# First attention of a five-phase layer kernel: output stored by batch, more key and square buffers, SP's queue from a list, new orders on all five engines

## The chip, the cores and the metric

The kernel runs on one NeuronCore of a Trainium2 chip. The metric is the time of one execution on the device in microseconds (us); lower is better. The engines are named as the profile names them: PE (matmul), DVE (VectorE), ACT (ScalarE), POOL (GpSimd), and SP, whose queue issues nearly all DMA transfers.

## The reference, cut to what matters

Two layers over 32 batches of 56 tokens with 256 features. Each layer is a cross-attention to a context of 1500 rows and a feed-forward part. The change touches the first attention alone:

```
q = (ln(x) @ Wq + bq)  -> 16 heads of 128, rmsnorm
k = (ctx @ Wk + bk)    ->  4 heads of 128, rmsnorm   (each serves 4 heads of q)
v = (ctx @ Wv + bv)    ->  4 heads of 128
probs = softmax(q k^T / sqrt(128) + mask)      # 56 x 1500 per head
x = x + (probs @ v) @ Wo
```

## The kernel before, in words

The phases run one after the other: queries of the first attention (`q0_phase`), the first attention itself (`attn0_phase`), its output projection with the router, the experts, the second attention and the last feed-forward part. Each phase ends with a barrier of all engines.

`attn0_phase` keeps float32 accuracy by splitting values into a high and a low float16 part; every product is then three matmuls (`three_products`, lines 111 to 113). A batch has 1500 context rows, held as 12 tiles of 125 rows. The attention does not project the values: it mixes the context rows themselves with the probabilities, and multiplies the result by Wv afterwards. The work is cut into steps with a letter and a number, and each engine has a list of these steps in `ORDER0`:

- `D0` to `D3`: a quarter of a batch's context is split; ACT writes the high part `ch` (line 713), POOL the low part `cl` (line 848).
- `K0` to `K11`: PE projects the keys of one context tile into a PSUM bank `ps_w`; DVE adds the bias and writes it to the key buffer `kb` (line 788).
- `q0` to `q11`: POOL squares a key tile into `ksq` (line 856). `Q0` to `Q5`: DVE sums the squares of two tiles (line 776). `N0` to `N5`: POOL takes the power -1/2 (lines 863 and 867) and scales the two key tiles in place (line 873).
- `R0` to `R11`: PE transposes a normalised key tile (line 899); ACT writes the high part `kTh` (line 718), DVE the low part `kTl` (line 794).
- `S0` to `S7`: for two heads at once PE makes the scores `ps_s`, DVE masks them and takes the maximum (line 806), ACT takes the exponential (line 728). `I`: DVE inverts the sum (lines 812, 815). `H`: ACT writes the high part of the probabilities `ph` (line 735). `L`: DVE writes the low part `pl` (line 820). SP then transposes both by DMA (line 627) to `pTh` and `pTl`.
- `P0` to `P23`: PE mixes the context; six steps make one group of four heads, each step is 12 matmuls. `G0` to `G3`: ACT (line 741) and DVE (line 826) split the result.
- `O0` to `O3` on PE, `Z0` to `Z3` on ACT (line 747) and DVE (line 830): multiplication by Wv, bias, and the output tile `ot`.

`rounds` walks such a list once per turn. In turn b the attention steps belong to batch b (with `<` to batch b-1) and the key steps `K`, `R`, `q`, `Q`, `N` to batch b+1, `D` to batch b+2; `>` means one batch later still. So while PE attends to one batch it prepares the keys of the next. Turns come in a hardware loop of six, four passes of it, with the turns before and after written out.

SP's queue has no list: `step` (lines 641 to 668) issues per turn the 16 transposes of the probabilities, four pairs of context loads (`load_ctx`, lines 582 and 583), the transposes of the context in two halves (`turn_ctx`, line 597), their store for the second attention (`keep_ctx`, line 606), the loads of the queries (`load_q`, line 616) and, every second turn, the store of the output (line 634). SP waits in the order of this code: an instruction whose data is late holds all that stand behind it.

The output tile `ot` holds the outputs of two batches, interleaved so that a row of it is one run of memory. There is one such tile, so `Z0` of an even batch waits until the store of the pair before it has landed. `kb` has four tiles: `K` of tile n waits for `R` of tile n-4. `ksq` has two: `q` of a new pair waits until DVE has summed the pair before.

Of the kernel before, what the change touches and what calls it, by code (L numbers as in the profile page):

```python
# [12 lines left out]
ds = bass.ds  # L13
# [157 lines left out]
def q0_phase(nc, g, io):  # L171

    with phase(nc) as (ctx, a):
# [304 lines left out]
def rounds(eng, steps, attend, work):  # L478

    def turn(batch):  # L480
        for kind, n, off in steps:
            lead = {"D": 2, "K": 1, "R": 1, "q": 1, "N": 1, "Q": 1}.get(kind, 0)
            at = moved(batch, off + lead)
            if exists(at, B):
                (work if lead else attend)(kind, n, at)

    count = (B - 4) // ROUND
    for b in (-2, -1, 0):
        turn((b, b % ROUND, b // ROUND))
    with eng.Fori(0, count) as i:  # L490
        for k in range(1, ROUND + 1):
            turn((ROUND * i + k, k % ROUND, i + k // ROUND))
    for b in range(ROUND * count + 1, B + 1):
# [13 lines left out]
def attn0_phase(nc, g, io):  # L507
# [6 lines left out]
    HT = KT // 2  # L514
    PS = 256.0
    PW = 2 * RP
    with phase(nc) as (ctx, a):
# [28 lines left out]
        ot = a.sb("a_ot", [128, 2, NH, 2, S], F16)  # L546
# [12 lines left out]
        stored = a.sem("a_stored")  # L559
# [6 lines left out]
        def _(sp):  # L566
# [52 lines left out]
            def turn(tile, r):  # L619

                G, h, k = tile[0], r // 2, r % 2
                wait(sp, s["mix_done"], NKV * G + h - 1)
                passed(sp, sp_gate)
                for n, (p, pT, ready) in enumerate(((ph, pTh, "p_hi"), (pl, pTl, "p_lo"))):
                    sp.wait_ge(s[ready], NR * G + r + 1)
                    passed(sp, sp_gate)
                    sp.dma_start_transpose(out=pT[:, h % 2, :, k], in_=p[:, k].rearrange("q k c -> q (k c)"))\
# [1869 lines left out]
```

## Time and profile before

| what | value |
|---|---|
| median of 3 runs | 4904.94 us (4901.27 to 4908.27) |
| profiled execution | 4904.49 us, its span 4902.4 us |
| busy over the span | PE 79%, DVE 72%, POOL 56%, ACT 49% |
| the first attention | about 280 us to 2719 us of the span |
| TensorE's granted clock, mean | 0.905 of full speed |

The profiled execution's own time is 2.1 us longer than its span, and 0.5 us below the median. PE's row of the profile is "3748999899899989999999720886159999999945": slices of 122.6 us with the busy share in tenths. The long stretch of 8 and 9 from the fourth slice on is the first attention. A matmul's span is modelled and runs into the next one's, so PE's idle time is best read from the views that name waits.

### The profile page before, as it was taken

What the parts mean: (1) busy time and instruction counts of PE and PEld (TensorE: products, weight loads), DVE (VectorE), ACT (ScalarE), POOL (GpSimd) and SP (SyncE); (2) the same over time, 40 slices, a digit from 0 to 9 for tenths busy, and PEclk for the clock granted to TensorE, in tenths of its full rate; (3) what the DMA queues carried; (4) which work ended last, traced back from release to release, by engine and by line L of the source; (5) the groups of instructions that cost most, each with busy time, mean ns of one, the idle gap of its engine ahead of it and who ended that gap; (6) DMA issues with size and microseconds to landing.
All of it is one profiled execution on the core that took longest, in us unless ns stands there. A gap on an engine that the chain in (4) does not pass through costs nothing. (4 is left out here: it accounts for less than half of the span.)

```text
span 4902.4 us, 104372 instructions
## 1 busy us (share of the span) xinstructions
PE 3888.0 (79%) x34578; PEld 2966.4 (61%) x34579; DVE 3509.9 (72%) x5413; ACT 2405.4 (49%) x3575; POOL 2762.2 (56%) x2176
## 2 busy tenths in 40 slices
PE   3748999899899989999999720886159999999945
PEld 2426777676677667677777710775137767677734
DVE  4847777777777777777777263344778888888967
ACT  1325555455455555555555113332137777777743
POOL 2566677676676666677774125334635555555532
PEclk9869999999999999999999965898579999999966
DMA  5246667677666666766775536555345444444410
GB/s 206 83 118 141 157 150 150 148 152 156 149 149 146 157 142 156 153 147 157 161 155 115 177 103 200 130 138 147 113 119 132 118 123 118 124 123 122 116 46 26
DMA packets 1276100, 664.62 MB, mean 136 GB/s; under 512 B 1095841, under 2 KB 1202977, under 8 KB 1271182
## 3 DMA queue, kind: packets, MB, share of 16 engines
q1 hardware_dynamic: 1247422, 617.09, 52.3%
q0 software_dynamic: 9216, 22.03, 1.4%
q10 hardware_dynamic: 19008, 19.40, 1.2%
q8 instruction: 290, 4.75, 0.4%
q14 instruction: 164, 1.34, 0.1%
HBM read 188.99 MB, written 146.01 MB: 68 GB/s over the span
## 5 line engine op out<-in xcount | busy, mean ns | idle before, releaser
L111 PE MATMUL a_pa<-a_pTh,a_ch 125*128 125x224 f16 x3072 | 802.2, 261 | 13.3 <-issue 11.2
L1896 POOL TENSOR_TENSOR b_pTl<-b_pe,b_pTh 125x1344 f16<-125x1344 f32 x192 | 539.5, 2810 | 483.6 <-ACT b_pTh L1955 460.2
L113 PE MATMUL a_pa<-a_pTh,a_cl 125*128 125x224 f16 x3072 | 802.1, 261 | 0.0
L112 PE MATMUL a_pa<-a_pTl,a_ch 125*128 125x224 f16 x3072 | 801.8, 261 | 0.0
L856 POOL TENSOR_TENSOR a_ksq<-a_kb 125x512 f32<-125x512 f32 x384 | 479.0, 1247 | 345.9 <-DVE a_kb L788 263.7
L873 POOL TENSOR_TENSOR a_kb<-a_kb,a_rk 125x512 f32<-125x512 f32 x384 | 546.3, 1423 | 68.8 <-POOL a_kb L873 34.5
L728 ACT ACTIVATE a_pr<-a_pr,a_nmax 112x1500 f32<-112x1500 f32 x256 | 395.4, 1545 | 322.5 <-DVE a_nmax L806 321.0
L735 ACT ACTIVATE a_ph<-a_pr,a_inv 112x1500 f16<-112x1500 f32 x256 | 396.4, 1548 | 285.9 <-DVE a_inv L815 285.8
L820 DVE SCALAR_TENSOR_TENSOR a_pl<-a_pr,a_inv,a_ph 112x1500 f16<-112x1500 f32 x256 | 480.9, 1878 | 67.0 <-ACT a_ph L735 66.5
L2001 DVE TENSOR_REDUCE b_mx<-b_ps 112x3 f32<-112x1500 f32 x256 | 439.1, 1715 | 96.3 <-PE b_ps L2078 94.9
L806 DVE CUSTOM_DVE_ANT_0 a_pr<-a_ps,a_mask 112x1500 f32<-112x1500 f32 x256 | 438.9, 1715 | 67.2 <-PE a_ps L113 58.5
L1948 ACT ACTIVATE b_pe<-b_pt 125x448 f32<-125x448 f32 x768 | 393.4, 541 | 165.0 <-PE b_pt L2100 159.7
L899 PE MATMUL a_pw<-ident,a_kb 125*128 125x125 f32 x1536 | 237.7, 278 | 153.8 <-POOL a_kb L873 113.0
L1955 ACT ACTIVATE b_pTh<-b_pe 125x1344 f16<-125x1344 f32 x256 | 337.0, 1317 | 5.0 <-PE b_po L2116 1.8
L867 POOL TENSOR_TENSOR a_rk<-a_rk,mhalf 125x8 f32<-125x8 f32 x192 | 318.5, 1659 | 35.2 <-POOL a_rk L863 35.2
L776 DVE TENSOR_REDUCE a_ssk<-a_ksq 125x8 f32<-125x1024 f32 x192 | 234.1, 1219 | 143.5 <-POOL a_ksq L856 142.5
L788 DVE SCALAR_TENSOR_TENSOR a_kb<-a_pw,a_bk 125x512 f32<-125x512 f32 x384 | 263.7, 687 | 101.9 <-PE a_pw L899 50.5
L111 PE MATMUL a_pw<-a_wk,a_cT 128*128 128x512 f16 x768 | 300.3, 391 | 45.5 <-DMA a_cT<-a_cl 39.5
L718 ACT ACTIVATE a_kTh<-a_pw 128x500 f16<-128x500 f32 x384 | 224.6, 585 | 210.9 <-PE a_pw L899 209.2
L111 PEld LDWEIGHTS a_pa<-a_pTh,a_ch 125*128 125x128 f16 x3072 | 302.3, 98 | 40.9 <-issue 12.2
L794 DVE TENSOR_TENSOR a_kTl<-a_pw,a_kTh 128x500 f16<-128x500 f32 x384 | 257.1, 670 | 92.1 <-ACT a_kTh L718 92.1
L112 PEld LDWEIGHTS a_pa<-a_pTl,a_ch 125*128 125x128 f16 x3072 | 303.0, 99 | 32.1
(381 smaller groups left out, 10918.9 us busy)
## 6 DMA issues: line engine op xcount, KB each, us to landing
b_ks<-b_kn SPq DMA_DIRECT2D x768, 93.8 KB
scratch_cT<-a_cT SPq DMA_DIRECT2D x64, 768.0 KB, 3.9
b_cT<-scratch_cT SPq DMA_DIRECT2D x32, 1536.0 KB
a_ctx<-ctx SPq DMA_DIRECT2D x128, 360.0 KB
scratch_yd<-e_y SPq DMA_DIRECT2D x88, 256.0 KB
scratch_xd<-q_zero ACTq DMA_DIRECT2D x4, 4736.0 KB
scratch_oT<-a_ot SPq DMA_DIRECT2D x16, 896.0 KB, 5.3
m_oT<-scratch_oT SPq DMA_DIRECT2D x16, 896.0 KB
```

The source lines that it names most:

```text
L111: nc.tensor.matmul(out, a_hi, b_hi, start=start, stop=False)
L112: nc.tensor.matmul(out, a_hi, b_lo, start=False, stop=False)
L113: return nc.tensor.matmul(out, a_lo, b_hi, start=False, stop=stop)
L728: nc.scalar.activation(pr[:, n % 2], pr[:, n % 2], ACT.Exp, scale=-1.0, bias=nmax[:, par, n:n + 1], accum_out=rsum[:, par, n:n + 1]).then_ ...
L735: nc.scalar.activation(ph[:, n % 2, :, 0:KP], pr[:, n % 2].rearrange("p (k c) -> p k c", c=KP), ACT.Copy, scale=inv[:, par, n:n + 1]).then ...
L806: nc.vector.tensor_tensor_reduce(out=pr[:, n % 2].rearrange("p (a k) -> p a k", k=500), in0=ps_s[0:RP, :, 0:500], in1=mask[:].rearrange("p ...
L820: nc.vector.scalar_tensor_tensor(pl[:, n % 2, :, 0:KP], pr[:, n % 2].rearrange("p (k c) -> p k c", c=KP), inv[:, par, n:n + 1], ph[:, n % ...
L856: nc.gpsimd.tensor_tensor(ksq[:, n % 2], kb[0:KP, n % 4], kb[0:KP, n % 4], ALU.mult).then_inc(s["k_squared"], 1)
L873: nc.gpsimd.tensor_tensor(k4, k4, rk[:, 1, NKV * t:NKV * t + NKV].unsqueeze(2) .to_broadcast([KP, NKV, HD]), ALU.mult).then_inc(s["k_norme ...
L1896: nc.gpsimd.tensor_tensor(pTl[:, n % 2, :, 0:RP], pe_[:, n % NP], pTh[:, n % 2, :, 0:RP], ALU.subtract).then_inc(s["l_pool"], 1)
L1948: nc.scalar.activation(pe_[:, r % NP, 4 * third:4 * third + 4], ps_t[at % 2][0:KP, 0:4 * RP].rearrange("p (k c) -> p k c", c=RP), ACT.Exp) ...
L2001: nc.vector.tensor_reduce(mx[:, par, n], ps_s[0:RP, :, 0:500], AX.X, ALU.max).then_inc(s["max_ready"], 1)
```

## The change

Four things, all in the first attention:

- `ot` becomes two tiles, one for even and one for odd batches, each with the semaphore `stored[par]`. The store is issued for every batch. A batch's 56 tokens are half of a run of 112 in memory, so its store writes 4096 runs of 56 float16 values (112 bytes) where the store of a pair wrote 128 runs of 3584 values.
- `kb` gets six tiles instead of four, `ksq` four instead of two; the waits follow (`n >= KBN`, and `k_ssq` one pair back).
- SP's code is replaced by a list `"sync"` that `rounds` walks: `h`, `l` are the transposes of the high and low probabilities, `c` a quarter of a context load, `x` the transposes of half a context, `k` its store, `q` the loads of the queries, `o` the store of a batch's output. The lists of the other four engines are new too.
- At the start, DVE and no longer POOL clears `ch` and `cl`, before it splits the weights; SP does not wait for the clearing before it loads context; ACT waits for the first tile cleared alone and no longer for the mask. `rounds` writes out three more turns at the start and enters the loop at turn 3 instead of turn 1; it still makes four passes of six.

```diff
 ORDER0 = {
     "tensor": """
-        P17< K0 S0 K1 P18< S1 P19< K2 K3 S2 R0 O2< P20< P21< P22< K4 K5 P23< R1 S3 P0 R2 P1 P2 P3 K6 P4 R3 K7
-        S4 R4 P5 K8 S5 K9 P6 R5 S6 P7 P8 P9 P10 O3< R6 K10 O0 K11 R7 S7 P11 R8 P12 P13 R9 P14 P15 P16 O1 R10
-        R11""",
+        K0 S0 K1 K2 S1 P17< P18< K3 S2 K4 P19< P20< P21< R0 K5 O2< P22< R1 P23< S3 R2 P0 P1 K6 P2 R3 K7 S4 K8
+        P3 P4 R4 S5 P5 K9 S6 R5 P6 P7 P8 R6 K10 O3< P9 P10 K11 S7 P11 R7 R8 P12 P13 O0 P14 P15 R9 P16 R10 R11
+        O1""",
...
     "gpsimd": """
-        D0 D1 N2 q6 D2 q7 D3 N3 q8 q9 N4 q10 q11 N5 q0> q1> N0> q2> q3> N1> q4> q5>""",
+        D0 D1 N2 q6 q7 D2 D3 q8 N3 q9 N4 q10 q11 N5 q0> q1> q2> N0> q3> q4> N1> q5>""",
+    "sync": """
+        h0 l0 h1 l1 h2 l2 c2 c3 x0 h3 l3 c0> k0 c1> h4 l4 h5 l5 o0< x1 q0> h6 l6 h7 k1 l7""",
 }
...
-    count = (B - 4) // ROUND
-    for b in (-2, -1, 0):
+    count = (B - 6) // ROUND
+    for b in range(-3, 3):
         turn((b, b % ROUND, b // ROUND))
...
-        kb = a.sb("a_kb", [128, 4, KVW])
-        ksq = a.sb("a_ksq", [KP, 2, KVW])
+        kb = a.sb("a_kb", [128, KBN, KVW])
+        ksq = a.sb("a_ksq", [KP, 4, KVW])
...
-        ot = a.sb("a_ot", [128, 2, NH, 2, S], F16)
+        ot = a.sb("a_ot", [128, 2, 2, NH, S], F16)
...
+            def store(tile):
+
+                G = tile[0]
+                par, pair = of_two(tile)
+                sp.wait_ge(s["o_taken"], NKV * G + NKV)
+                passed(sp, sp_gate)
+                with nc.allow_non_contiguous_dma(reason="56 tokens of a pair's 112"):
+                    sp.dma_start(io.oT[ds(pair, 1), :, :, :, S * par:S * par + S].rearrange("a p n h q -> p (a n h) q"),
+                                 ot[:, par].rearrange("p n h q -> p (n h) q")).then_inc(stored[par], 16)
...
-            act.wait_ge(s["cleared"], 4)
+            act.wait_ge(s["cleared"], 1)
...
-                    if n == 0 and batch[1] % 2 == 0:
-
-                        wait(act, stored, 16 * half)
+                    if n == 0:
+
+                        wait(act, stored[par], 16 * half)
...
-            act.wait_ge(s["placed"], 1)
...
         def _(dve):
-            for t in (ph, pl):
+            for t in (ch, cl):
                 nc.vector.memset(t[:], 0.0).then_inc(s["cleared"], 1)
...
+            for t in (ph, pl):
+                nc.vector.memset(t[:], 0.0).then_inc(s["cleared"], 1)
...
-                    if n >= 4:
-                        dve.wait_ge(s["work_done"], NW * G + AT["R", n - 4] + 1)
+                    if n >= KBN:
+                        dve.wait_ge(s["work_done"], NW * G + AT["R", n - KBN] + 1)
...
-            for t in (ch, cl):
-                nc.gpsimd.memset(t[:], 0.0).then_inc(s["cleared"], 1)
+            pool.wait_ge(s["cleared"], 2)
...
-                    wait(pool, s["k_ssq"], KT // 2 * G + n // 2)
+                    wait(pool, s["k_ssq"], KT // 2 * G + n // 2 - 1)
```

POOL, in the turns written out at the start, from `q6` of a batch to the scaling of its fourth pair (`a_ksq<-a_kb` is a `q`, `a_cl` a `D`, and `N` begins with `a_rk<-a_ssk`). Before:

```order
L856 TENSOR_TENSOR a_ksq<-a_kb 125x512
L848 TENSOR_TENSOR a_cl<-a_ctx,a_ch 125x768
L856 TENSOR_TENSOR a_ksq<-a_kb 125x512
L848 TENSOR_TENSOR a_cl<-a_ctx,a_ch 125x768
L863 TENSOR_SCALAR a_rk<-a_ssk 125x8
L867 TENSOR_TENSOR a_rk<-a_rk,mhalf 125x8
L873 TENSOR_TENSOR a_kb<-a_kb,a_rk 125x512 x2
L856 TENSOR_TENSOR a_ksq<-a_kb 125x512 x2
```

The same place after the change:

```order
L820 TENSOR_TENSOR a_ksq<-a_kb 125x512 x2
L812 TENSOR_TENSOR a_cl<-a_ctx,a_ch 125x768 x2
L820 TENSOR_TENSOR a_ksq<-a_kb 125x512
L827 TENSOR_SCALAR a_rk<-a_ssk 125x8
L831 TENSOR_TENSOR a_rk<-a_rk,mhalf 125x8
L837 TENSOR_TENSOR a_kb<-a_kb,a_rk 125x512 x2
L820 TENSOR_TENSOR a_ksq<-a_kb 125x512
```

The two squares of a pair now stand together, and the first square of the following pair stands ahead of the pair's own scaling.

SP's queue around the store of the output, between the transposes for `h5`, `l5` and what follows them. Before (a turn that stores):

```order
L606 DMA scratch_cT<-a_cT 256x1x1536
L634 DMA scratch_oT<-a_ot 128x3584
L627 DMA_TRANSPOSE a_pTh<-a_ph 128x12x112
L627 DMA_TRANSPOSE a_pTl<-a_pl 128x12x112
L582 DMA a_ctx<-ctx 120x768
L583 DMA a_ctx<-ctx 5x768
```

After the change (every turn):

```order
L640 DMA scratch_oT<-a_ot 4096x1x56
L600 DMA_TRANSPOSE a_cT<-a_ch 128x12x128
L600 DMA_TRANSPOSE a_cT<-a_cl 128x12x128
L619 DMA a_qh<-scratch_qh 128x896
L619 DMA a_ql<-scratch_ql 128x896
L630 DMA_TRANSPOSE a_pTh<-a_ph 128x12x112
L630 DMA_TRANSPOSE a_pTl<-a_pl 128x12x112
```

The context's second half and the queries now stand between the store and the transposes of the last two pairs of heads, and the store has 4096 rows of 56 values.

## Rows read from the trace of the kernel before

**Rows 1.** Busy time by stretch: the steady part, and the first keys
```profile
core 0: us, PE busy (x) PEld busy (x) DVE busy (x) ACT busy (x) POOL busy (x), PEclk, DMA share, GB/s
500.00:2500.00 2000.00, 1832.19 (x13671) 1395.33 (x13670) 1516.28 (x2117) 1049.11 (x1303) 1386.47 (x1087) 0.99 0.68 152
...
313.00:377.00 64.00, 38.62 (x127) 17.60 (x127) 22.46 (x30) 10.12 (x16) 42.53 (x40) 0.66 0.48 122
```
**Rows 2.** What PE waited for from 500 to 2500 us: total, times, longest
```profile
PE a_pw L899 <- POOL a_kb L873: 88.7, 51, 4.2
PE a_pw L899 <- DVE a_kb L788: 25.4, 14, 2.9
PE a_ps L111 <- DVE a_nmax L806: 24.2, 27, 1.2
PE a_po L111 <- DVE a_ot L830: 13.5, 25, 0.6
PE a_pa L111 <- issue: 11.2, 3, 3.8
```
**Rows 3.** PE in order of time, one stretch of a turn
```profile
1011.67 0.26 PE L111 MATMUL a_pa<-a_pTh,a_ch 125*128 125x224 f16 x1
...
1016.17 0.26 PE L113 MATMUL a_pa<-a_pTh,a_cl 125*128 125x224 f16 x1
...
1016.84 0.59 PE L899 MATMUL a_pw<-ident,a_kb 125*128 125x125 f32 x4
1017.27 0.38 PE L111 MATMUL a_pw<-a_wk,a_cT 128*128 128x512 f16 x1
...
1018.35 0.38 PE L113 MATMUL a_pw<-a_wk,a_cT 128*128 128x512 f16 x1
```
**Rows 4.** Groups from 500 to 2500 us: count, busy us, mean ns, idle before
```profile
L111 PE MATMUL a_pa<-a_pTh,a_ch 125*128 125x224 f16 x2600 | 678.9, 261 | 11.2 <-issue 11.2
L873 POOL TENSOR_TENSOR a_kb<-a_kb,a_rk 125x512 f32<-125x512 f32 x326 | 469.4, 1440 | 58.4 <-POOL a_kb L873 29.4 <-POOL a_rk L867 29.1
L856 POOL TENSOR_TENSOR a_ksq<-a_kb 125x512 f32<-125x512 f32 x327 | 408.2, 1248 | 299.3 <-DVE a_kb L788 227.0 <-POOL a_kb L873 39.1 <-POOL a_ksq L856 26.0
```
**Rows 5.** Other engines' waits from 500 to 2500 us
```profile
POOL a_rk L863 <- DVE a_ssk L776: 175.3, 111, 2.3
...
ACT a_ot L747 <- DMA scratch_oT<-a_ot: 62.0, 14, 5.6
```
**Rows 6.** Issues of single lines on the queues: duration ns min/median/max
```profile
L627 SPq DMA_TRANSPOSE a_pTl<-a_pl x256: 1301/1343/2245, 387.6 to 2698.0; - x128
...
L634 SPq DMA_DIRECT2D scratch_oT<-a_ot x16: 343/386/403, 574.1 to 2713.6; - x16
...
L1832 SPq DMA_DIRECT2D scratch_o<-b_ot x64: 818/942/1151, 3692.3 to 4722.3; - x64
...
L262 ACTq DMA_DIRECT2D scratch_xd<-q_zero x4: 460/13268/18067, 4.1 to 35.5; - x4
```
**Rows 7.** DMA queues and issues from 500 to 2500 us; KB each, us to landing
```profile
q1 hardware_dynamic: 806706, 301.78, 67.9%
...
scratch_oT<-a_ot SPq DMA_DIRECT2D x14, 896.0 KB, 5.3
...
a_pTl<-a_pl SPq DMA_TRANSPOSE x218, 3.1
```
**Rows 8.** The start of the phase in order of time: POOL, DVE, SP, PE
```profile
280.03 7.78 POOL L840 MEMSET a_ch<- 128x9216 f16 x1 [10.86 <-POOLq L139]
...
280.43 1.34 DVE L756 MEMSET a_ph<- 112x1536 uint32 x1 [5.29 <-PEq L139]
...
295.62 0.32 SPq L582 DMA_DIRECT2D a_ctx<-ctx  x1
...
306.14 2.12 SPq L597 DMA_TRANSPOSE a_cT<-a_ch  x1
...
313.10 0.59 PE L111 MATMUL a_pw<-a_wk,a_cT 128*128 128x512 f16 x1 [39.48 <-DMA a_cT<-a_cl]
```

More of the change, by code:

```diff
@@ L485, in turn @@
                 (work if lead else attend)(kind, n, at)
[L487 to L488 removed]
+    count = (B - 6) // ROUND
+    for b in range(-3, 3):
         turn((b, b % ROUND, b // ROUND))
     with eng.Fori(0, count) as i:
[L491 removed]
+        for k in range(3, ROUND + 3):
             turn((ROUND * i + k, k % ROUND, i + k // ROUND))
[L493 removed]
+    for b in range(ROUND * count + 3, B + 1):
         turn((b, b % ROUND, b // ROUND))
@@ L558, in attn0_phase @@
         turned = [[a.sem(f"a_turned{n}{i}") for i in range(2)] for n in "hl"]
-        stored = a.sem("a_stored")
+        stored = [a.sem(f"a_stored{i}") for i in range(2)]
         names = ("scores_done nmax_ready exp_done p_hi p_lo mix_done mix_hi mix_lo values_done o_hi o_taken inv_scaled "
@@ L617, in load_q, with turn @@
                                  o[ds(G, 1), :, :].rearrange("a p n -> p (a n)")).then_inc(q_in[par], 16)
-            def turn(tile, r):
+            def turn(tile, r, n):
                 G, h, k = tile[0], r // 2, r % 2
+                p, pT, ready = ((ph, pTh, "p_hi"), (pl, pTl, "p_lo"))[n]
                 wait(sp, s["mix_done"], NKV * G + h - 1)
                 passed(sp, sp_gate)
[L624 to L627, printed above, removed]
-                        .then_inc(turned[n][k], 16)
@@ L684, in _ @@
-            for p in range(2):
-                load_ctx(at(2), p)
-            count = (B - 4) // ROUND
-            step(at(0))
-            with sp.Fori(0, count) as i:
-                for k in range(1, ROUND + 1):
-                    step((ROUND * i + k, k % ROUND, i + k // ROUND))
-            for b in range(ROUND * count + 1, B):
-                step(at(b))
-            store(NT - 1)
-            sp.wait_ge(stored, 16 * NT)
+                sp.wait_ge(s[ready], NR * G + r + 1)
+                passed(sp, sp_gate)
@@ new lines, in send @@
+            def send(kind, n, tile):
+                if kind in "hl":
+                    turn(tile, n, "hl".index(kind))
+                elif kind == "c":
+                    load_ctx(tile, n)
+                elif kind == "x":
+                    turn_ctx(tile, n)
+                elif kind == "k":
+                    keep_ctx(tile, n)
+                elif kind == "q":
+                    load_q(tile)
+                else:
+                    store(tile)
+            rounds(sp, order["sync"], send, send)
```

82 lines of the change are left out of this document (19 added, 63 removed).

## The prediction

> **What bounds the kernel now.** I read the busy time by stretch first, to see which engine is full in the long steady part of the first attention. From 500 to 2500 us PE is busy 1832 of 2000 us, DVE 1516, POOL 1386 and ACT 1049, at a granted clock of 0.99 [rows 1]. A batch needs 96 mixing products of each of the three kinds, and 2600 of one kind ran in the stretch [rows 4], so it holds 27.1 batches: one takes 73.9 us, of which PE is idle 6.2 us. PE is the bound, and 6.2 us is all that an order can win there.
>
> The view of PE's waits says where these 6.2 us lie [rows 2]. The largest part is the transposes of keys (line 899): 88.7 us for a key that POOL had not scaled yet, and 25.4 us for DVE's copy of a projection. The scores wait 24.2 us for DVE's maximum, the output step 13.5 us for DVE's last read. The 11.2 us of "issue" come three times, about 3.7 us each, once in some 440 us: the edge of the six-turn loop.
>
> PE in order of time gives the lengths of its steps without waits [rows 3]. From 1011.67 to 1016.17 lie 47 starts of mixing products, 0.096 us each, so a `P` of 12 takes 1.15 us and an `O` of 6 takes 0.57 us; a transposed tile 0.43 us; a `K` of 6 products, 0.216 us apart, 1.29 us. An `S` of 9 products of 500 columns is taken at the same rate less a little, 1.90 us. A turn is 24 P, 12 K, 8 S, 12 R and 4 O: 27.6 + 15.5 + 15.2 + 5.2 + 2.3 = 65.8 us.
>
> **The steady turns.** PE's own work stays as it is. What changes is when each key is ready. POOL had its own two waits: it waited 175.3 us, 6.5 us a batch, for DVE's sum of squares [rows 5], because `N` stood right behind the two squares that it needs; and 227.0 us for DVE's copies of keys [rows 4]. With four square tiles the next pair's square stands between, and with six key tiles `K` can run further ahead of `R`. POOL's busy time is 51.2 us a batch [rows 1], and some 40 instructions with 0.18 us between them (58.4 us ahead of 326 scalings [rows 4]) make it 59 us: it fits into 66 us, but without much room.
>
> I laid the new lists side by side, with PE's lengths above and for POOL 1.25 us for a square and 1.44 us for a scaling [rows 4], and asked for each `R` whether its key is there when PE comes to it. All are there 2 us early or more, except R6 (about 1 us), R10 (about 1.3 us) and R11 (at the same moment). So the 88.7 + 25.4 = 114.1 us of waits go, 4.2 us a batch. The 65 waits also hide a modelled tail of the last matmul each, 0.26 us of span where starts lie 0.096 apart, 0.17 us: another 0.4 us a batch. DVE and POOL will slip against my walk in places, and I charge 0.5 us a batch for the three tight keys. The waits for the maximum and for the output, 1.4 us a batch, and the loop's edge stay. Net 4.1 us a batch. The bounds are 1.0 us (POOL's hand-offs come back at other keys) and 6.0 us (all but the loop's edge goes).
>
> **The two output tiles.** ACT waited 62.0 us in 14 pairs for the store to land, 4.4 us each [rows 5]. Behind it on ACT stand the copies of transposed keys, and behind these DVE's copy of a projection, the second wait of rows 2. The new wait is for the store of two batches before, a whole turn old. This is part of the 25.4 us above and is not counted again.
>
> **The store itself** is the added cost. It goes from 128 runs a pair to 4096 runs of 112 bytes a batch, and no row shows such a store. On SP the old one issues in 0.39 us; a store of 448 runs of 64 bytes in the second attention issues in 0.94 us [rows 6]. The slope is 1.74 ns a run, so 4096 runs keep the queue 7.1 us. At the upper end stands ACT's clearing of a buffer with 4736 runs: 13.3 us for an issue that follows another [rows 6], 2.8 ns a run, 11.5 us here. At the lower end stands one issue, 0.4 us. I take 7.1 us, the slope of stores of short runs. On the DMA engines a packet takes 26.9 ns on average (67.9% of 16 times 2000 us over 806,706 packets) [rows 7], so the store adds up to 6.9 us of all 16 and the share rises from 0.68 to about 0.82.
>
> Queued behind the store are the second half of the context, the queries, and the transposes for the last two pairs of heads. In my walk the store can go 52.6 us after the turn's first `K`. With T for the store, 3.7 us for two transposes of the context (1.85 us each, an estimate between the 2.12 us of [rows 8] and the 1.34 us of the smaller ones [rows 6]), 0.8 us for two plain loads, four transposes of 1.35 us [rows 6], 0.6 us for the context's store and the rest of 3.1 us to landing [rows 7], the last low part lands at 65 + T. PE needs it for P18 at 65.8 + 8.8 = 74.6 us, or 77.8 with the waits that stay. T may be 10 to 13 us before PE waits; at 7.1 us nothing is lost, at 11.5 us 0 to 2 us a turn.
>
> One rule speaks against this store: the Trainium skill, "DMA: Bandwidth & Descriptors", section Specifications, wants at least 512 bytes a run for full rate, and says that the engine reads, modifies and writes below it. No row shows that for this store; the 64-byte runs of rows 6 issue at the slope I use. If it doubled my upper bound, T would be 23 us and the result that of the last rival below.
>
> **The start.** SP's first context load stood at 295.62 us, behind two clearings of 7.78 us by POOL; the first transpose followed at 306.14 and PE's first key product at 313.10 [rows 8]. DVE clears 1536 words in 1.34 us, so the 4608 words of `ch` or `cl` take 4.0 us each and both are clear at about 288.6. The load now overlaps this. I take 13 us (bounds 7 us, the earlier clearing alone, and 16 us). Then the first batch's keys, 64 us in which POOL is busy 42.5 us [rows 1], lose the wait for sums (175.3 us in 111 times, 1.6 us each, less a gap of 0.2 us) in five of six pairs: 7 us [rows 5]. Together 20 us. At the end the last store has more runs and nothing to hide it: 3 us lost.
>
> **Sum.** 30 turns have both kinds of work: 30 x 4.1 = 123 us, plus 20, less 3: 140 us. The profiled execution takes 4904.5 us (0.5 us below the median): 4764 us. On its own this case reaches from 4725 to 4805 us.
>
> **Rivals.**
> - Everything falls into place: all of PE's waits but the loop's edge go, 6.0 us a turn. 180 + 20 - 3 = 197 us, 4708 us. For it: in my walk only three keys are tight. Against: DVE is at 56 us of work a batch, and the scores' hand-off through one PSUM tile stays.
> - POOL becomes the second bound. With DVE denser, POOL's operations stretch (1.25 us in the mean for a square [rows 4]), R6, R10 and R11 come late and half of the gain is new waits: 1.9 us a turn, 57 + 15 - 3 = 69 us, 4836 us.
> - The lists bring nothing: the waits move from one key to another, as many as before, and the start gives back what it wins. 4905 us.
> - Slower: the store holds SP's queue so long that PE waits at P18 for the last transposes in each turn. This decides from T = 13 us; from T = 17 us a turn is longer than now. With T = 20 us PE waits 7 us and loses 2.9 us net a turn: +87 - 20 = +67 us, 4972 us. For it: 32 times the runs on a queue whose engines are two thirds busy. Against: the slope of rows 6.
>
> **How the numbers follow.** Forecast 0.55, the better case 0.12, POOL 0.20, nothing 0.05, the store 0.08. The range from 4710 to 4850 us takes in the first three nearly whole, 0.85, and leaves out the last two. A measurement of this kernel can tell about 0.2%, 10 us, from no change. Faster by more: 0.88; within: 0.04; slower by more: 0.08.
>
> **What would show it.** In the profile after, from 500 to 2500 us: about 28.7 batches (2750 mixing products of a kind), PE busy near 97%; the transposes' wait for POOL's keys below 30 us; no wait of ACT for the output's store; POOL busy 74%. The store's issue on SP with what stands behind it shows T. PE's first key product near 300 us. Wrong if PE waits for a DMA `a_pTl<-a_pl` in steady turns, or if POOL's scaling still leads PE's waits.

## The result and the profile after

The changed kernel takes 4854.25 us (median of 4 runs, 4847.24 to 4860.74), the kernel before, beside it, 4906.33 us. The ratio is 0.9895, 95% interval 0.9876 to 0.9914: about 52 us faster, where the prediction had 140, and 4 us above its range.

The page's busy line, the steady stretch and the first keys by stretch (columns as in [rows 1]), and PE's waits from 500 to 2500 us, as in [rows 2]:

```profile
PE 3880.9 (80%) x34578; PEld 2964.0 (61%) x34579; DVE 3529.1 (73%) x5415; ACT 2403.6 (50%) x3575; POOL 2784.4 (57%) x2174
```
```profile
500.00:2500.00 2000.00, 1879.41 (x14036) 1432.66 (x14033) 1572.21 (x2173) 1076.09 (x1337) 1451.34 (x1114) 0.99 0.84 156
307.00:371.00 64.00, 39.70 (x138) 18.52 (x137) 23.47 (x32) 10.13 (x16) 43.65 (x41) 0.70 0.51 133
```
```profile
PE a_pw L863 <- POOL a_kb L837: 54.6, 31, 1.9
PE a_pw L111 <- DVE a_kTl L759: 40.0, 27, 1.5
PE a_ps L111 <- DVE a_nmax L771: 15.1, 6, 2.6
PE a_pw L111 <- issue: 9.6, 3, 3.5
PE a_pa L111 <- DMA a_pTl<-a_pl: 0.3, 1, 0.3
```

PE is busy 94% of the stretch (92% in [rows 1]), not 97%. Of the waits of [rows 2], that for POOL's scaled key fell from 88.7 to 54.6 us and that for the maximum from 24.2 to 15.1; those for DVE's copy of a projection and for the output are gone. In their place stands one that was small, 40.0 us for DVE's low part of the transposed keys. Before, it was:

```profile
PE a_pw L899 <- DVE a_kTl L794: 4.9, 3, 1.7
```

POOL waits less for the sums of squares, and ACT's wait for the store is gone ([rows 5] had 175.3 and 62.0). The groups say how much ran, as in [rows 4]: 2672 mixing products, 27.8 batches (27.1 before).

```profile
POOL a_ksq L820 <- DVE a_kb L753: 240.4, 109, 8.6
POOL a_rk L827 <- DVE a_ssk L741: 91.2, 83, 1.5
```
```profile
L111 PE MATMUL a_pa<-a_pTh,a_ch 125*128 125x224 f16 x2672 | 692.8, 259 | 0.5 <-DMA a_pTl<-a_pl 0.3
L837 POOL TENSOR_TENSOR a_kb<-a_kb,a_rk 125x512 f32<-125x512 f32 x334 | 470.9, 1410 | 59.6 <-POOL a_rk L831 29.8 <-POOL a_kb L837 29.8
```

The store, with its issue on SP (duration in ns, min, median, max), then the queue and the landings (columns as in [rows 7]), and SP's queue behind one store in order of time:

```profile
L640 SPq DMA_DIRECT2D scratch_oT<-a_ot x32: 553/597/613, 491.3 to 2655.0; - x32
```
```profile
q1 hardware_dynamic: 939152, 308.98, 83.4%
...
scratch_oT<-a_ot SPq DMA_DIRECT2D x27, 448.0 KB, 9.6
a_pTl<-a_pl SPq DMA_TRANSPOSE x223, 3.3
```
```profile
1142.70 0.61 SPq L640 DMA_DIRECT2D scratch_oT<-a_ot  x1
1143.70 5.37 SPq L600 DMA_TRANSPOSE a_cT<-a_ch  x1
1149.11 2.81 SPq L600 DMA_TRANSPOSE a_cT<-a_cl  x1
```

The start in order of time, against [rows 8]. ACT's first copy waits for the context's load, which took 10 us where it took 4 before:

```profile
280.28 3.90 DVE L719 MEMSET a_ch<- 128x4608 uint32 x1 [5.91 <-issue]
...
282.10 0.32 SPq L585 DMA_DIRECT2D a_ctx<-ctx  x1
...
292.56 0.84 ACT L677 ACTIVATE a_ch<-a_ctx 125x768 f16<-125x768 f32 x1 [7.27 <-DMA a_ctx<-ctx]
...
306.61 0.58 PE L111 MATMUL a_pw<-a_wk,a_cT 128*128 128x512 f16 x1 [33.75 <-DMA a_cT<-a_cl]
```

**Where the time went.** I take the starts of DVE's maximum for the first pair of heads of each batch, `S0`; two neighbours bound a turn. There are 31 turns from batch 0 to batch 31. A jump is the place where the loop of six turns goes back to its start; a fall is a stretch in which PE's granted clock is 0.50 of full speed; a quiet turn has neither.

| stretch | before, us | after, us | gained | predicted |
|---|---|---|---|---|
| up to `S0` of batch 0 | 379.3 | 370.9 | 8.4 | 20 |
| 31 turns | 2271.3 | 2218.1 | 53.2 | 123 |
| from there to the next phase | 68.8 | 76.3 | -7.5 | -3 |

The turns missed most of it. Some of them by stretch (columns as in [rows 1]), first two turns of the kernel before (one in which ACT has waited for the store, a quiet one) and the pair of turns at a jump back of its loop; then a turn of the changed kernel with a fall of the clock, a quiet one, and its pair at a jump:

```profile
1114.26:1188.32 74.06, 66.81 (x506) 51.08 (x505) 55.59 (x79) 38.52 (x48) 51.04 (x40) 1.00 0.70 156
1188.32:1259.80 71.48, 66.72 (x506) 51.08 (x505) 55.71 (x78) 38.74 (x48) 51.02 (x40) 1.00 0.65 151
...
812.86:967.84 154.98, 138.04 (x1010) 104.20 (x1009) 111.88 (x157) 77.31 (x96) 102.49 (x80) 0.96 0.66 145
```
```profile
511.57:583.06 71.49, 68.20 (x506) 51.75 (x505) 55.74 (x78) 38.63 (x48) 52.90 (x40) 0.98 0.80 154
654.65:724.53 69.88, 66.51 (x505) 51.17 (x504) 56.42 (x78) 38.63 (x48) 52.12 (x40) 1.00 0.82 155
937.97:1091.16 153.19, 137.19 (x1010) 103.35 (x1009) 113.74 (x156) 77.17 (x96) 104.28 (x80) 0.98 0.79 142
```

The first and the last turn apart there are 29. Three pairs stand at jumps: 463.5 us before, 460.6 after, 2.9 us gained. The other 23, called ordinary here, took 1668.8 us (72.55 each) and now 1621.2 (70.49), 47.6 us gained. The rest, 3 us, is the first turn. So the pair at a jump takes some 154 us in both kernels, and eight of the 23 turns take 71.5 us where a quiet one takes 69.9. All of them have the wait of 1.83 to 1.86 us for the last key; in those eight the granted clock then falls to 0.50, the lower level of 1.2 GHz, for 3.4 us: the products of a key after it start every 0.43 us and not every 0.216. The kernel before has such a fall in five of its 23, so the falls are not new.

```profile
576.70 0.62 PE L863 MATMUL a_pw<-ident,a_kb 125*128 125x125 f32 x4 [1.86 <-POOL a_kb L837]
...
578.33 0.63 PE L112 MATMUL a_pw<-a_wk,a_cT 128*128 128x512 f16 x1
578.76 0.63 PE L113 MATMUL a_pw<-a_wk,a_cT 128*128 128x512 f16 x1
...
581.35 0.38 PE L111 MATMUL a_ps<-a_kTh,a_qh 128*112 128x500 f16 x1
581.56 0.37 PE L112 MATMUL a_ps<-a_kTl,a_qh 128*112 128x500 f16 x1
```

PE's waits, summed turn by turn, were 5.45 us in an ordinary turn before and are 3.35 us now. That is the 2.1 us by which an ordinary turn got shorter.

At the jump at 1007 us PE waits 3.0 us for its own instructions and DVE 4.9 (the first `S0` of the pass, from PE's and DVE's order of time), after which PE waits 2.4 us for DVE's maximum:

```profile
1007.38 0.40 PE L111 MATMUL a_pw<-a_wk,a_cT 128*128 128x512 f16 x1 [3.02 <-issue]
...
1017.39 0.42 PE L111 MATMUL a_ps<-a_kTh,a_qh 128*112 128x500 f16 x1 [2.37 <-DVE a_nmax L771]
```
```profile
1015.60 1.72 DVE L771 CUSTOM_DVE_ANT_0 a_pr<-a_ps,a_mask 112x1500 f32<-112x1500 f32 x1 [4.86 <-issue]
```

In the turn that starts there POOL waits 4.7 us for its instructions, and PE 1.1 us for a key and 2.6 for a maximum, neither of which it waits for in a quiet turn. These four waits of PE are 9.2 us; the clock is at 0.50 for 6.8 us in the pair, half of which is 3.4. Together that is 12.6 of the 13.4 us by which this pair exceeds two quiet turns. DVE's waits for instructions from 500 to 2500 us, before and after, show that the jumps did not stay as they were:

```profile
DVE a_pr L806 <- issue: 8.2, 3, 2.9
```
```profile
DVE a_pr L771 <- issue: 14.7, 3, 5.1
```

POOL's went from 8.6 to 14.1 us, PE's from 11.2 to 9.6.

### The profile page after: what moved, and what is told of

Same layout as the page of the kernel before. It is cut to its first block and busy times, and to the rows that moved or that the text cites. A ratio compares the mean times of both kernels' runs of the same rounds, so it can differ in the third digit from the quotient of the medians.

```text
span 4847.0 us, 104716 instructions
## 1 busy us (share of the span) xinstructions
PE 3880.9 (80%) x34578; PEld 2964.0 (61%) x34579; DVE 3529.1 (73%) x5415; ACT 2403.6 (50%) x3575; POOL 2784.4 (57%) x2174
## 5 line engine op out<-in xcount | busy, mean ns | idle before, releaser
L1860 POOL TENSOR_TENSOR b_pTl<-b_pe,b_pTh 125x1344 f16<-125x1344 f32 x192 | 540.2, 2813 | 484.2 <-ACT b_pTh L1919 460.6
L837 POOL TENSOR_TENSOR a_kb<-a_kb,a_rk 125x512 f32<-125x512 f32 x384 | 538.9, 1403 | 68.8 <-POOL a_rk L831 34.6
L785 DVE SCALAR_TENSOR_TENSOR a_pl<-a_pr,a_inv,a_ph 112x1500 f16<-112x1500 f32 x256 | 498.9, 1949 | 46.7 <-ACT a_ph L699 45.8
L111 PEld LDWEIGHTS a_pa<-a_pTh,a_ch 125*128 125x128 f16 x3072 | 300.7, 98 | 24.6 <-issue 5.4
L111 PE MATMUL a_ps<-a_kTh,a_qh 128*112 128x500 f16 x768 | 293.8, 383 | 21.3 <-DVE a_nmax L771 20.4
L759 DVE TENSOR_TENSOR a_kTl<-a_pw,a_kTh 128x500 f16<-128x500 f32 x384 | 256.3, 674 | 72.1 <-ACT a_kTh L682 71.9
```

Of the source, the lines that this page charges most:

```text
L111: nc.tensor.matmul(out, a_hi, b_hi, start=start, stop=False)
L785: nc.vector.scalar_tensor_tensor(pl[:, n % 2, :, 0:KP], pr[:, n % 2].rearrange("p (k c) -> p k c", c=KP), inv[:, par, n:n + 1], ph[:, n % ...
L837: nc.gpsimd.tensor_tensor(k4, k4, rk[:, 1, NKV * t:NKV * t + NKV].unsqueeze(2) .to_broadcast([KP, NKV, HD]), ALU.mult).then_inc(s["k_norme ...
L1860: nc.gpsimd.tensor_tensor(pTl[:, n % 2, :, 0:RP], pe_[:, n % NP], pTh[:, n % 2, :, 0:RP], ALU.subtract).then_inc(s["l_pool"], 1)
```

## The experiments

Chips differ outside the first attention. In the traces from two of the chips used, the experts' first product waits 172 to 177 us for its input, and in all others 196 to 202 us, whatever the kernel. In the runs of this table the kernel before took 4873 to 4876 us on the first two chips and 4901 us on a third. Each ratio is against the kernel before on the same chip; beside it stand the 31 turns, and what follows them in the phase, from one trace of each kernel.

| kernel | ratio to before (95%) | 31 turns, us | behind them, us |
|---|---|---|---|
| before | 1 | 2271.3 | 68.8 |
| changed, first trace | 0.9895 (0.9876 to 0.9914) | 2218.1 | 76.3 |
| changed again | 0.9897 (0.9881 to 0.9914) | 2211.4 | 74.0 |
| e1, store in whole runs | 0.9938 (0.9921 to 0.9955) | 2218.0 | 68.2 |
| e2, old lists, whole runs | 1.0002 (0.9992 to 1.0011) | 2242.7 | 66.2 |
| e3, old lists, short runs | 0.9957 (0.9940 to 0.9973) | 2244.8 | 71.9 |
| e4, new lists, pair store | 0.9877 (0.9860 to 0.9893) | 2207.8 | 69.1 |
| e5, no loop | 0.9818 (0.9801 to 0.9834) | 2184.0 | 75.5 |
| e6, later keys | 0.9940 (0.9923 to 0.9956) | 2246.1 | 74.5 |
| e7, context first | 0.9888 (0.9871 to 0.9904) | 2217.6 | 76.2 |
| e8 = e4 + e5 + e7 | 0.9796 (0.9779 to 0.9812) | 2184.0 | 68.3 |
| e9, before without loop | 0.9872 (0.9856 to 0.9889) | 2213.5 | 66.8 |
| e10, last key later | 0.9858 (0.9842 to 0.9875) | 2196.1 | 71.7 |
| e11, each store twice | 1.0330 (1.0313 to 1.0347) | 2409.8 | 90.5 |
| e12 = e8 + e10 | 0.9702 (0.9686 to 0.9718) | 2142.5 | 67.8 |
| e13 = e5 + e10 | 0.9723 (0.9707 to 0.9740) | 2143.0 | 74.3 |
| e14 = e3 without loop | 0.9816 (0.9800 to 0.9833) | 2187.3 | 71.9 |
| e15 = e12, second attention without loop too | 0.9576 (0.9559 to 0.9593) | 2142.0 | 68.2 |

### The store and the output tiles

e1: the scratch by batch, the short runs moved to the projection's load.
```diff
-sp.dma_start(io.oT[ds(pair, 1), :, :, :, S * par:S * par + S].rearrange("a p n h q -> p (a n h) q"), ...)
+sp.dma_start(io.oT[ds(pair, 1), :, par].rearrange("a p n h q -> p (a n h q)"), ...)
```


> The changed kernel, but the scratch of the outputs is laid out by batch, so that each store has 128 whole runs of 3584 bytes in place of 4096 runs of 112; the output projection's load takes the short runs instead (two loads a tile). Theory A (the short runs load the DMA engines, and what goes through these engines behind them, the instructions of the loop's edge and of the written-out turns among it, comes late): the share of the DMA engines from 500 to 2500 us falls from 0.84 to about 0.70, the loop's edge costs 8 us again and not 14, written-out turns take 70 us and not 71.5, and the first attention ends 25 to 45 us earlier than in the changed kernel. Theory B (the edge and the written-out turns are slow because of how the new lists cut the loop): only the share falls; edges stay at 14 us, written-out turns at 71.5, and the first attention ends within 10 us of the changed kernel's.

e2 and e3: the kernel before with `ot[:, par]`, `stored[par]` and a store for each batch, in 128 whole runs (e2) or in 4096 short ones (e3).

> The kernel before, with two output tiles and a store per batch of 128 whole runs (scratch laid out by batch as in e1); lists and all else as before. Both theories: ACT's wait of 62 us for the store goes, and with it most of PE's 25 us of waits for DVE's copies; 10 to 30 us faster than before, inner turns 72.5 us, edges 8 us.

> The kernel before, with two output tiles and the change's store per batch in 4096 runs of 112 bytes; lists as before. Against e2 only the runs differ. Theory A: the attention ends 15 to 45 us later than in e2, edges of about 14 us, share of the DMA engines about 0.80. Theory B: within 5 us of e2 in spite of the share.

e4: the changed kernel with one tile and the old store.
```diff
-ot = a.sb("a_ot", [128, 2, 2, NH, S], F16)
+ot = a.sb("a_ot", [128, 2, NH, 2, S], F16)
```


> The changed kernel with the old store: one output tile for a pair, 128 runs of 7168 bytes every second turn. Theory A: edges 8 us, written-out turns about 70, ACT waits for the store about 4 us in 14 pairs, and the sum is still 10 to 30 us faster than the changed kernel. Theory B: edges stay at 14 us, ACT's wait comes on top: 0 to 30 us slower than the changed kernel.

The main queue from 500 to 2500 us (packets, MB, share) and the store's size and landing, of e1, e2 and e3:

```profile
q1 hardware_dynamic: 830360, 308.18, 73.0%
...
scratch_oT<-a_ot SPq DMA_DIRECT2D x27, 448.0 KB, 3.1
```
```profile
q1 hardware_dynamic: 820966, 306.34, 68.8%
...
scratch_oT<-a_ot SPq DMA_DIRECT2D x28, 448.0 KB, 3.7
```
```profile
q1 hardware_dynamic: 931442, 306.10, 79.5%
...
scratch_oT<-a_ot SPq DMA_DIRECT2D x28, 448.0 KB, 9.8
```

Theory A falls. In e1 the share fell by ten points and the pair at a jump still took 151 to 153 us, with eleven turns of 71.5 us where the changed kernel had eight; the 31 turns are 2218.0 us, and the time behind them fell from 76.3 to 68.2. In the old lists the short runs cost 2.1 us in 31 turns and 5.7 us behind them. So one store in short runs costs next to nothing in the turns, and 6 to 8 us at the end. The ratios of e1 and e2 are worse for what comes after the first attention: from its end to the experts' first product they take 360 and 361 us, where e3, on the same chip, takes 330. These two alone load the output projection's input in short runs. So e2, for which 10 to 30 us were expected, ends the first attention 32 us earlier than the kernel before and gains nothing in all. Of the 30 us, 12 show in PE's later wait for `m_xs`, which DVE makes (0.6 us in e3, 12.6 in e2 and 13.1 in e1); PE's first wait there is 21 to 22 us in all three.

e3 and e2 gain 26 to 29 us in the turns over the kernel before: that is the output tiles' part, since the lists are the old ones. e4 has the new lists and no second tile, and is no slower in the turns (2207.8) than the changed kernel (2211.4 to 2218.1): ACT's wait for the store, which both theories expected, is nowhere in its trace. The two parts overlap.

The jumps stayed at 151 to 154 us a pair in all four. DVE's and POOL's waits for instructions there are 7.9 and 8.8 us in e2, 8.0 and 9.0 in e3, as before: what made them longer in the changed kernel comes with the new lists and buffers, not with the tiles or the runs. Lists, key tiles and square tiles were never tried apart from each other.

### The loop's edge

The changed kernel unaltered stands beside e5 to e7:

> The changed kernel, unaltered, as the level on this chip for the three runs beside it. Every theory: ratio to the kernel before as measured first, 0.99, the first attention ends near 2665 us, turns of the loop 69.9 or 71.5 us, two turns at an edge together near 153 us.

e5 writes all turns out; e9 does the same to the kernel before (and to SP's `step`).
```diff
-    with eng.Fori(0, count) as i:
-        for k in range(3, ROUND + 3):
-            turn((ROUND * i + k, k % ROUND, i + k // ROUND))
-    for b in range(ROUND * count + 3, B + 1):
+    for b in range(-3, B + 1):
         turn((b, b % ROUND, b // ROUND))
```


> The changed kernel with all turns of the first attention written out, no loop. The theory of the edge (at the loop's edge each engine waits some 3 to 5 us for its instructions, one after the other along the chain, and the two turns there take 153 us whichever lists run): three visible edges of 13 us go, 35 to 40 us faster than the changed kernel. The rival (written-out turns are slow by themselves, 71.5 us for 69.9, because their instructions are fetched): the edges go, but 18 turns get 1.6 us longer, 0 to 15 us faster in all.

> The kernel before with all turns of the first attention written out, no loop. The theory of the edge: an edge costs the kernel before 8 us over its own turns (155 us for two turns of 73.4) and the changed kernel 13 to 14 us over its (153 for two of 69.9), so writing out gives 24 us here, 39 there, and without loops the lists gain some 15 us more than they did with them: 4845 to 4855 us here. The rival (written-out turns of the old lists are faster in themselves, 71.3 for 73.4, as the profile of before shows at both ends of the loop): 50 to 70 us faster than before, 4805 to 4822, and the lists gain 25 to 40 us without loops, less than with them.

e5 gained what its theory had: 0.0079 of 4873, 39 us. In the traces its 31 turns are 34 us shorter than in the changed kernel's first trace and 27 us shorter than in the repeat's, which was the fastest of that kernel's four executions. No turn of it is longer than 71.5 us, and DVE's and POOL's waits for instructions (14.7 and 14.1 us in three pieces in the changed kernel) are gone. But fifteen of its turns have a fall, where the changed kernel has eight ordinary ones and its repeat five. e9 was 63 us faster than before, which was the rival's figure: besides the jumps that went, its turns took 71.5 us where ordinary ones had taken 72.6. So without loops the changes of this kernel are worth 0.9872 less 0.9818, 26 us, half of what they are with them. Why the old lists run better written out is only half seen: PE waits once a turn for POOL in e9 (44.9 us in 28) and twice in the loop [rows 2]. At the last key it waits for DVE's low part there, 41.8 us in 26, and not for POOL. Whether a jump sets the engines in places from which they don't return, or a turn in the loop is slower by its register instructions, was not tried.

### The last key, and the fall of the clock

e6:
```diff
-K0 S0 K1 K2 S1 P17< P18< K3 ... R6 K10 O3< P9 P10 K11 S7 ... P15 R9 P16 R10 R11 O1
+K0 S0 K1 K2 S1 P18< K3 ... R6 K10 O3< P9 K11 P10 S7 ... P15 R9 P16 P17 R10 R11 O1
```


> The changed kernel with PE's list alone altered: K11 one product group earlier, and the next-to-last R and the last R behind P17, so that the last key is asked for 2.3 us later after its projection. Theory C (PE's wait of 1.85 us for POOL's last key is the work that I had put down as ready at the same moment, and the fall of the granted clock to 0.50 for 3.3 us comes right behind it, which is what makes 71.5 us of a turn of 69.9): the wait falls below 0.5 us a turn, the turns behind which no fall comes take 68.2 to 68.8 us, and the 71.5 us turns are gone; 40 to 60 us faster. The rival (the wait moves to another key or to DVE's copy, since DVE and POOL set the pace): turns stay within 0.5 us of 69.9.

e10:
```diff
-K0 S0 K1 K2 S1 P17< P18< K3 ... P15 R9 P16 R10 R11 O1
+K0 S0 K1 K2 S1 P18< K3 ... P15 R9 P16 R10 P17 R11 O1
```


> The changed kernel, PE's list with P17 of the batch before the last R and not behind S1 (K11 stays where it was, unlike e6). Theory C (the 1.85 us for the last key are PE's and can be covered by P17's 1.15 us, the loss in e6 came from K11's move, which made PE wait for DVE's copies): the wait falls to about 0.7 us a turn, quiet turns take 68.8 us, 15 to 35 us faster. The rival (the pace is set by DVE and the two projection banks, PE's wait moves on as in e6): quiet turns 69.5 to 71 us, 0 to 25 us slower.

PE's waits from 500 to 2500 us, e6 and then e10:

```profile
PE a_pw L111 <- DVE a_kTl L759: 83.8, 52, 2.7
...
PE a_pw L863 <- POOL a_kb L837: 1.5, 3, 0.6
```
```profile
PE a_pw L111 <- DVE a_kTl L759: 38.7, 28, 1.5
PE a_pw L863 <- POOL a_kb L837: 21.8, 32, 0.9
...
PE a_pa L111 <- DMA a_pTl<-a_pl: 5.7, 8, 1.6
```

e6 went the way of its rival and further: the last key's wait vanished, PE's wait for DVE's low parts, which free the two projection banks, rose from 40.0 to 83.8 us, and quiet turns took 70.6 us. Before `K11` PE now waits 2.5 to 2.7 us in each turn, where it waited 1.4 to 1.5, and the clock falls at this wait in 17 of the 23 ordinary turns. In these turns it falls no more behind `R11`, though the two last transposes still stand side by side there. e10 leaves `K11` alone and puts one group of products, 1.15 us, ahead of the last key. The wait fell from 1.86 to 0.7 us a turn, and no ordinary turn has a fall, where the changed kernel had eight and its repeat five. The 31 turns are 15 to 22 us shorter. The quiet turns did not shorten in the loop (69.8 us where 68.8 was expected, as its rival had it: a wait of 0.4 us for DVE's low part came back, and some turns wait for a transpose by DMA); in the written-out turns at the start and the end they are 69.2. The fall went with the wait: gone where e10 shortened it, moved where e6 moved it. Why the same wait brings one in some turns and not in others is not shown.

### The start

e7 issues the first two context loads ahead of the weights.
```diff
+for p in range(2):
+    sp.dma_start(cx[0:120, p], src[0:120]).then_inc(ctx_in[p], 16)
+    sp.dma_start(cx[120:KP, p], src[120:KP]).then_inc(ctx_in[p], 16)
 for n, w in enumerate((io.Wk, io.Wv)):
     sp.dma_start(wst[:, n], ...)
```


> The changed kernel with the first batch's first two context loads issued ahead of the weights and the mask. Theory D (ACT's first copy of the context waits 7.3 us for a load that stands behind the weights and the mask on the queue): ACT's first copy moves from 292.6 to about 286, POOL's first subtraction to 288.5 to 290, and PE's first key product from 306.6 to 301 to 303; 3 to 6 us faster in all. The rival (the rest of the chain is slower, or the weights now come late): the first key product stays within 1.5 us of 306.6.

ACT's first copy moved to 288.2 us (286 was expected) and PE's first key product to 301.6 us, as expected; `S0` of batch 0 stood at 364.4 us, against 372.5 in the repeat of the changed kernel. The whole was the same within the interval (0.9888 against 0.9897), and the turns had more falls of the clock (nine ordinary ones against five), which took 6 us of it back. In e8 the product stood at 302.7 us but in e12 and e15, with the same order, at 307.1 and 306.6. ACT's first copy stands at 292.0 and 290.5 us there, and POOL's second low part took 4.3 us in place of 2.4. The gain is not there in each trace; why was not tried.

### A store twice

e11 issues each store a second time, to a scratch of its own.
```diff
-sp.dma_start(io.oT[...], ot[:, par]...).then_inc(stored[par], 16)
+for o in (io.oT, io.oT2):
+    sp.dma_start(o[...], ot[:, par]...).then_inc(stored[par], 16)
```


> The changed kernel with each store of a batch's outputs issued twice (the second to a scratch of its own): 8192 short runs a turn. It measures what the store has to spare. From the two shares (0.68 and 0.84) a store takes about 11 us of 16 engines a turn, so the share goes to 0.95 or more. As the prediction had it (the transposes behind the store may be 10 to 13 us late before PE waits, one store delays them by 3 us): turns stay at 69.9 or 71.5 us, 0 to 10 us slower, all at the end. The rival (the engines are nearly full and everything behind the store waits): PE waits for the transposes' DMA in each turn, 2 to 8 us a turn, 60 to 250 us slower.

Its stretch, PE's first wait and SP's queue behind the two stores:

```profile
500.00:2500.00 2000.00, 1789.32 (x12773) 1334.17 (x12772) 1437.86 (x1981) 977.05 (x1216) 1314.36 (x1014) 0.94 0.89 148
```
```profile
PE a_pa L111 <- DMA a_pTl<-a_pl: 103.2, 25, 5.8
```
```profile
1120.52 3.91 SPq L641 DMA_DIRECT2D scratch_oT<-a_ot  x2
1124.84 9.10 SPq L600 DMA_TRANSPOSE a_cT<-a_ch  x1
1133.98 1.58 SPq L600 DMA_TRANSPOSE a_cT<-a_cl  x1
```

The rival was right, though the share rose to 0.89 and not to 0.95. A turn takes 78.4 us: PE waits 4.1 us in each for the transposes behind the stores, and the clock falls behind that wait (0.94 in the mean). One store in short runs has room before this happens, a second has not. This is the last rival of the prediction, made true by doubling its cause.

### Together

> What helped, together: the changed kernel with the old store (one output tile, a pair in 128 runs), all turns written out, the first two context loads first. If the parts add: e5's gain over the changed kernel (39 us), the end's 5 to 7 us (the last store lands after 4 us and not 9), the start's 5 us: 4765 to 4780 us on this chip, ratio to before 0.978 to 0.981. The rival (the clock's falls take the small gains back, since a turn of 69.7 becomes one of 71.4): within 6 us of e5, 4777 to 4789.

> What helped, with e10's list: pair store, all turns written out, two context loads first, P17 before the last R. If they add: e8's ratio 0.9796 less the clock's falls, of which 18 a run cost 1.65 us each, and less 0.4 us a turn of waiting: 0.971 to 0.974. The rival (a wait moves to DVE's copies, as the 69.9 us turns of e10 show): 0.975 to 0.979.

> The changed kernel with e10's list and all turns written out; store in short runs and the start as in the changed kernel. Theory: e10's gain with the loop (0.4%) grows to 25 to 35 us without it, since the turns between falls make up more of the run; ratio 0.974 to 0.977 and no steady turn of 71.4 us. If the short runs matter now that PE reaches P17 earlier (e10 showed 5.7 us of waits for a transpose), e13 is 10 to 20 us behind e12; if only the last store's landing and the start count, 10 us. Rival (the falls of the clock come back at another wait): ratio as e5, 0.982.

> The kernel before with two output tiles, the store by batch in short runs, and all turns written out: what is left of the output tiles' gain when the loop is gone. Against e9 (0.9872). If the tiles' gain is ACT's wait alone (every second turn 1.5 to 2.9 us longer where the edge sets the engines' places, 0.9 us in e9): turns of 70.9 throughout, 10 to 20 us less than e9, ratio 0.983 to 0.985. If the edge alone had made that wait costly: within 6 us of e9, less 5 us for the last store's landing.

The steady stretch of e12 and PE's waits in it:

```profile
500.00:2500.00 2000.00, 1934.65 (x14566) 1473.76 (x14564) 1597.28 (x2256) 1109.55 (x1385) 1515.48 (x1154) 1.00 0.75 160
```
```profile
PE a_pw L111 <- DVE a_kTl L759: 38.4, 28, 1.7
PE a_pw L863 <- POOL a_kb L837: 20.7, 30, 0.7
```

e12 and e13 have 29 turns of 69.1 to 69.8 us and no fall of the clock from batch 1 to batch 31, PE busy 97%. e8 without e10's list gained nothing over e5 in the turns (2184.0 both, 15 falls in each); its 11 us are the start and the end. So the parts do not add: the list alone (e10) is worth 0.4%, the loop alone (e5) 0.8%, both together (e13) 1.7%. With the loop the list took away five to eight falls and left quiet turns at 69.8 us; without it the same list takes away fifteen falls (1.65 us each, 25 us) and shortens quiet turns from 69.7 to 69.2 us. e12 and e13 came out better than expected by 0.1 to 0.2%. e12 is 0.2% below e13 (the intervals overlap): its pair store lands sooner, 67.8 us behind the last turn against 74.3. e14 says two things. Against e9 the output tiles are worth 0.0056, 27 us, without the loop too, more than the 10 to 20 us that were expected: turns of 70.9 and 71.8 us by turns became 70.6 to 71.1 throughout. Against e5 it says what the rest of the change brings when there is no loop, start and new lists with their buffers: nothing that the ratio can tell (0.9816 against 0.9818). In the turns it is 3.3 us: e5's quiet turn is 0.9 us shorter than e14's 70.6, 28 us in all, and its fifteen falls, of which e14 has none after batch 1, take 25 us back.

> e12 with the second attention's loop of two turns written out as well, on all its engines. In the changed kernel PE waits 33.2 us there in 12 pieces for its own instructions (2.8 us each), one at each edge. If an edge costs as much more than PE's own wait as in the first attention (13 us for 3.3 us of PE's wait): up to 100 us faster than e12. If only PE's wait goes: 30 us, ratio 0.964. Rival (the second attention's edges are hidden behind another engine): ratio 0.970 as e12.

e15 beats all of them at 4697 us: PE's 33 us of waits for instructions in the second attention's loop of two turns are gone, and from its first store to its last it takes 971 us in place of 1027 (issues at 3551.8 and 4523.2, against 3524.9 and 4552.0 in e12). That is 56 us for 33 us of PE's own waits: there too a jump costs more than PE waits for its instructions. The ratio says 0.0126 of 4901, 62 us.

## Why the prediction was wrong, by its steps

- **What bounds the kernel**: right. PE is the bound. A quiet turn of the changed kernel takes 69.9 us, where the prediction had 73.9 less 4.1, 69.8. That agreement is luck: the prediction's terms leave 67.3 us of busy PE and 2.5 of waits, where the quiet turn has 66.5 and 3.4.
- **30 x 4.1 = 123 us**: this is the step that failed; the turns gave 53, 70 us less. Two things are wrong in it.
  - One price for all turns, with "the loop's edge stays" taken as 3.7 us of PE's. The stretch behind the 73.9 us holds all three jumps, and the two turns at a jump last 154 us before and after: 2.9 us gained in these six turns, not 24.6. Waits of PE went there too, but DVE's and POOL's waits for instructions grew from 8.2 and 8.6 us to 14.7 and 14.1. This makes 22 us. e5 took 39 us away by removing the jumps alone, though its turns have more falls.
  - The waits of an ordinary turn. They were 5.45 us before, where the prediction's mean has 5.8 without the edge, and 3.35 us are left, not 2.1. The 0.4 us for modelled tails did not show: PE is busy 67.1 us in an ordinary turn, before and after. So 2.1 us were gained for 4.1, which makes 47 us in 23 turns. The last us or so is in the first and the last turn.
  - The view that would have shown the jumps was at hand, the span turn by turn. It reads 71.5, 73.0, 73.4, 74.1 and 80 in the kernel before, with granted clocks of 1.00, 0.98 and 0.96. It shows the clock too, which was not in the sum: eight ordinary turns cost 1.6 us more each, 13 us, but the kernel before has five such turns, so that only three of them, 5 us, are a loss against it.
- **The three tight keys**: R11, "at the same moment", is late by 1.83 to 1.86 us in every turn but the last; R6 and R10 are not. The 0.5 us charged for them was too small, and the 1.4 us that should stay (maximum and output) went, and a wait of 1.5 us on DVE's low part came that my walk did not have: 3.4 us of waits are left in a quiet turn, where the prediction's terms left 2.1.
- **The output tiles**: counted as part of the same 25.4 us of waits. e3 shows 26 us for them alone in the old lists, e4 nothing in the new ones: not an addition, as the prediction said.
- **The store, T = 7.1 us**: harmless, as predicted, though T is made differently. SP's issue takes 0.60 us, and the delay lies in the transposes behind it: 5.61 and 2.81 us in the median, where e1, whose store has whole runs, has 1.50 and 1.89. From the store's issue to the end of the second transpose it is 9.67 us against 4.46, so T is about 5 us. The share rose to 0.84 where I had 0.82. From e2 to e3 the share of the queue went up by 10.7 points for 28 stores with 3968 more runs each: 0.107 x 32,000 / 111,100 = 31 ns a run, the 26.9 ns of [rows 7] and somewhat more. The room behind it was put too high, at 10 to 13 us: with two stores the pieces shown for e11 give 3.91 + 9.10 + 1.58 - 3.7 = 10.9 us, and PE already waits 4.1 us a turn. The room is then near 7 us, an estimate from these two numbers.
- The Trainium skill, "DMA: Bandwidth & Descriptors", section Specifications, asks for 512 bytes a run. The runs agree on the direction: the same 448 KB land after 9.8 us in runs of 112 bytes and after 3.7 us in runs of 3584. But a rule on the rate of a transfer did not decide here; what stands behind it in the queue and how much room that has did.
- **The start, 20 us**: 8.4. The first key product came 6.5 us earlier, below the lower bound of 7, since the load of the context, issued 13.5 us earlier, stood close behind the weights and the mask and landed after 10 us, not after 4; e7 shows this. The first batch's keys gained 1.9 us and not 7: PE's wait for POOL in them went from 19.3 to 14.1 us, but its wait for DVE's low part from 4.6 to 9.9.
- **The end, -3 us**: -7.5 (-5.2 in the repeat). The landing takes 9.4 us and not 5.3; e2 and e3, which up to there differ in the runs alone, are 5.7 us apart.
- **Rivals**: none as written. The nearest in time is POOL as second bound at 4836 us, with 57 us in the turns where 53 were measured. That is mostly luck: R11 did come late, but R6 and R10 did not, POOL's square still takes 1.24 us in the mean, POOL is busy 73% and PE's wait for it fell. What kept the turns' gain down is in good part at the jumps, which it left alone. Of the two marks of failure the second came true: POOL's scaling still leads PE's waits.

The Trainium skill, "TensorE: Matmul & The Clock Gate", section "HAM oscillation — how this bites in real kernels", prices a fall at half of the time at the lower clock. The trace agrees: 3.4 us at 0.50 make a turn 1.6 us longer (71.49 against 69.88 us, with waits of 3.2 and 3.4 us).

## What to carry to other kernels

Read a loop's span turn by turn before pricing an order, sum the waits of an ordinary turn, and price the turns at a jump by themselves: a mean turn spreads the jumps' waits over all turns, and here they did not shrink with the order. On PE a wait of 1.9 us just ahead of dense products can cost 1.6 us more through the clock, so a small wait in each turn is worth moving work of its own size in front of it. Changes that each touch the same slack (buffers, order, loop, clock) are to be tried together as well as alone: here 0.4% and 0.8% made 1.7%.

## What was not expected of the hardware

- A jump back costs more than any engine's own wait for instructions: PE 3.0 to 3.5 us, DVE 4.9, POOL 4.7, and the pair of turns 13 to 14 us over two quiet ones. DVE's and POOL's waits were 2.7 and 2.9 us each in the kernel before; why the new lists make them longer is open.
- A turn has two lengths, 69.9 and 71.5 us, that each repeat for several turns (in e5 four of 71.4 follow three of 69.7). With P17 ahead of the last key (e10, and e12, e13 and e15 without the loop) only the short one is left.
- 4096 runs of 112 bytes issue in 0.60 us, where 448 runs of 64 bytes took 0.94 [rows 6]: the number of runs did not set the issue. The cost shows on the next transpose of the queue.
